# Unread TensorE products ahead of some stages in the first five and last four tiles of an RWKV and FP4 kernel

## What is computed

```python
h = _layernorm(x) * (1 + ca) + sa
for i in range(2):                              # _forward, two layers
    h = h + _time_mix(_ln(h, ln1_w), p)         # five mixes, r k v w g, a scan over tokens (wkv), group norm, Wo
    h = h + _channel_mix(_ln(h, ln2_w), p)      # relu(k @ cWk)^2 @ cWv, gated by sigmoid(r @ cWr)
x = x + ga * _ln(h, ln_out_w)
h = _layernorm(x) * (1 + cb) + sb
gate, y = fp4_linear(h, w_gate), fp4_linear(h, w_up)
x = x + gb * fp4_linear(silu(gate) * y, w_down) # operands quantized in blocks of 16
```

## Time and profile before

| | us |
|---|---|
| median of three runs | 3195.91 |
| lowest and highest | 3187.82, 3196.2 |
| the profiled execution, its own time | 3192.44 |
| its span, first to last instruction | 3190.7 |
| mean granted TensorE clock | 0.969 of full speed |

### The profile page before, as it was taken

The page is one execution under the profiler, slowest core; times in us unless marked ns, Lnnn a source line. Parts: engine busy times, 40 slices in busy tenths (PEclk is TensorE's granted clock), DMA queues, the critical chain, the costliest instruction groups (busy, mean ns, idle before and its releaser), DMA issues.

```text
span 3190.7 us, 79561 instructions
## 1 busy us (share of the span) xinstructions
PE 2926.2 (92%) x33341; PEld 2317.9 (73%) x33341; DVE 2383.7 (75%) x5345; ACT 1252.3 (39%) x2451; POOL 1270.3 (40%) x1456
## 2 busy tenths in 40 slices
PE   5589999999999999999999999999999999999875
PEld 3467777777777777777777777777777777777653
DVE  4646777887777788777778787777878777787654
ACT  1233444444344434434443444444443444344321
POOL 3234344444344444433444443344444434444320
PEclk7689999999999999999999999999999999999987
DMA  4000000000000000000000000000000000000000
GB/s 140 13 5 8 8 8 12 9 11 12 12 8 8 12 8 12 12 12 11 6 11 8 12 12 12 12 5 12 8 12 12 11 12 8 8 8 12 8 8 7
DMA packets 36313, 41.56 MB, mean 13 GB/s; under 512 B 2748, under 2 KB 34680, under 8 KB 35960
## 3 DMA queue, kind: packets, MB, share of 16 engines
q1 hardware_dynamic: 35696, 36.32, 3.6%
q10 hardware_dynamic: 264, 0.16, 0.0%
HBM read 28.08 MB, written 8.39 MB: 11 GB/s over the span
## 4 chain that ended last, share of the span: by engine, by line
PE 67%; DVE 13%; issue 11%; POOL 7%; ACT 2%; DMA 0%; DVEq 0%; ACTq 0%; POOLq 0%
PE ps_all L1087 11%; PE ps_all L1309 10%; PE ps_all L1095 7%; PE ps_all L1276 6%; PE ps_all L1290 6%; PE ps_all L1199 6%; PE ps_all L1328 5%; PE ps_all L1079 3%; PE ps_all L1126 2%; DVE sxrk L954 2%; POOL grstd L605 2%; DVE att L961 2%; PE ps_all L1320 2%; PE ps_all L1173 1%; POOL sxrk L568 1%
## 5 line engine op out<-in xcount | busy, mean ns | idle before, releaser
L581 POOL TENSOR_TENSOR mixin<-mixin,hT_tm 128x512 f32<-128x512 f32 x320 | 375.6, 1179 | 912.4 <-DVE mixin L920 910.3
L954 DVE TENSOR_TENSOR sxrk<-sxrk,dec 128x512 f32<-128x512 f32 x384 | 301.7, 786 | 217.0 <-PE ps_all L1199 214.4
L1276 PE MATMUL ps_all<-chan,cwk 128*128 128x256 f32 x1536 | 362.7, 386 | 3.0 <-DVE ffn_work L1015 3.0
L1290 PE MATMUL ps_all<-cwv,chan 128*128 128x256 f32 x1536 | 348.6, 383 | 0.0
L1199 PEld LDWEIGHTS ps_all<-sxrk 64*64 64x64 f32 x12288 | 223.0, 137 | 158.6 <-issue 158.4
L1199 PE MATMUL ps_all<-sxrk 64*64 64x32 f32 x12288 | 259.2, 223 | 72.0 <-DVE att L961 68.3
L1290 PEld LDWEIGHTS ps_all<-cwv,chan 128*128 128x128 f32 x1536 | 286.5, 190 | 41.7 <-DVE ffn_work L1015 1.0
L1276 PEld LDWEIGHTS ps_all<-chan,cwk 128*128 128x128 f32 x1536 | 284.7, 190 | 42.7 <-DVE ffn_work L1015 3.8
L920 DVE SCALAR_TENSOR_TENSOR mixin<-ps_all,vcol,sxrk 128x256 f32<-128x256 f32 x640 | 272.4, 476 | 25.6 <-PE ps_all L1130 14.6
L563 POOL TENSOR_TENSOR rstd<-var,powc 128x2 f32<-128x2 f32 x224 | 179.8, 803 | 201.5 <-DVE var L867 192.0
L961 DVE COPY_PREDICATED att<-masks,ps_all 128x256 f32<-128x256 uint8 x384 | 201.5, 525 | 9.3
(11 more groups left out here) (179 smaller groups left out, 6290.7 us busy)
## 6 DMA issues: line engine op xcount, KB each, us to landing
xin<-in_L_attn_x_dram SPq DMA_DIRECT2D x32, 256.0 KB, 2.7
tok<-in_L_attn_x_dram SPq DMA_DIRECT2D x32, 256.0 KB, 2.7
out_dram<-x SPq DMA_DIRECT2D x32, 256.0 KB, 2.1
cwk<-in_L_attn_cWk_dram SPq DMA_DIRECT2D x2, 768.0 KB, 7.9
cwv<-in_L_attn_cWv_dram SPq DMA_DIRECT2D x2, 768.0 KB, 10.0
ffn_work<-in_L_wmod_dram SPq DMA_DIRECT2D x2, 512.0 KB, 6.3
tok<-in_L_ffn_w_down_dram SPq DMA_DIRECT2D x1, 704.0 KB, 4.0
tok<-in_L_ffn_w_gate_dram SPq DMA_DIRECT2D x1, 640.0 KB, 7.6
```

The lines of the kernel that those rows point to most:

```text
L581: pool.tensor_tensor(m, m, hT["tm", l][:, :, :, 1:P + 1].rearrange("p k c t -> p (k c) t"), ALU.add).then_inc(ev["mixed"][b], 1)
L954: v.tensor_tensor(rko, rko, t, ALU.mult).then_inc(ev["rk_lev"][b], 1)
L1276: ins = pe.matmul(bank(b, "ck", lj, "k")[:, m * TT:(m + 1) * TT], cwk[:, l, k, n:n + P], k_in[:, k, :], start=(k == 0), stop=(k == KC - 1))
L1290: ins = pe.matmul(bank(b, "cv", l, "v")[:, c * D:(c + 1) * D], relu[t // 2][:, t % 2, c * P:(c + 1) * P], cwv[:, l, t, :], start=(t == 0), ...
```

## The change

`WAITING` names, for tiles 0 to 4 and for the last four, stages of PE and a number n for each. Before such a stage PE now waits for the bank as `fill` does and then issues n products of the 128 x 128 identity with itself into the first 128 columns of that bank. Nobody reads them: the stage that follows starts its own group in the same bank. For `lev.3`, `lev.5` and `lev.6` the bank is not the stage's own but that of `pg` or `kt`, the next stage that writes another bank. In all there are 659 such products: 144, 118, 67, 17 and 7 in tiles 0 to 4, and 4, 16, 93 and 193 in tiles 28 to 31. Nothing else is moved; the other engines' lists are the same.

```diff
+WAITING = {
+    0: """0 turn.tm 16; 0 mix 9; 0 mf.0 4; 0 pw1 7; 0 pk 2; ...
...
+    -1: """... 1 yt 12; 1 wo 8; ... 4 xt 61; 4 gu.0.0 3; 4 ht.0 23; 4 ht.1 23; 4 dn
...
-        def turns(eng, run, steps, meanwhile):
+        def turns(eng, run, steps, meanwhile, before=None):
             for i, b, kind, arg in run:
+                if before:
+                    before(i, b, kind, arg)
                 steps[kind](i, b, arg)
...
+            RESULT = {"lev.3": "pg", "lev.5": "kt", "lev.6": "kt"}
...
+            def unread(i, b, kind, arg):
+
+                name = stage_name(kind, arg)
+                n = count[i, b, name] if (i, b, name) in count else 0
+                if n:
+                    kind, arg, use = use_of[b, RESULT[name] if name in RESULT else name]
+                    fill(pe, i, b, kind, arg, use)
+                    for _ in range(n):
+                        pe.matmul(bank(b, kind, arg, use)[:, 0:P], ident[:, :], ident[:, :], start=True, stop=True)
...
-            turns(pe, RUN[PE], steps, meanwhile)
+            turns(pe, RUN[PE], steps, meanwhile, unread)
```

More of the change, by code:

```diff
@@ L45 @@
         4/4 dn; 0/0 mf.0; 4/3 lna.out; 1/2 st.0 st.1; 4/3 lna.ffn; 0/0 mf.1; 1/2 gnb; 0/0 mf.3""",
+}
+WAITING = {
+    0: """0 turn.tm 16; 0 mix 9; 0 mf.0 4; 0 pw1 7; 0 pk 2; 0 pr 3; 0 lev.3 4; 0 lev.5 5; 0 lev.6 3; 0 kt 2; 0 yt 11; 0 wo
+        7; 2 turn.cm 23; 2 ck.0 1; 1 pr 3; 1 lev.3 2; 1 lev.5 4; 1 lev.6 3; 1 kt 1; 1 yt 13; 1 wo 3; 3 turn.cm 8; 3 ck.0
+        3; 4 xt 3; 4 gu.0.0 1; 4 ht.0 2; 4 ht.1 1""",
+    1: """0 turn.tm 11; 0 mix 3; 0 mf.0 4; 0 pw1 4; 0 pk 13; 0 pr 3; 0 lev.3 3; 0 lev.5 5; 0 lev.6 3; 0 kt 2; 0 yt 11; 0
+        wo 3; 2 turn.cm 1; 1 pw1 13; 1 pr 3; 1 lev.3 2; 1 lev.5 4; 1 lev.6 3; 1 kt 1; 1 yt 13; 1 wo 3; 3 turn.cm 3; 3
+        ck.0 3; 4 xt 3; 4 gu.0.0 1""",
+    2: """0 turn.tm 1; 0 mix 3; 0 pw1 1; 0 pr 3; 0 lev.3 3; 0 lev.5 4; 0 lev.6 3; 0 kt 2; 0 wo 3; 1 turn.tm 2; 1 pw1 13; 1
+        pr 3; 1 lev.3 2; 1 lev.5 4; 1 lev.6 3; 1 kt 1; 1 yt 13; 1 wo 3""",
[4 rows of a table added]
+    -2: """1 turn.tm 2; 1 pw1 13; 1 pr 3; 1 lev.3 3; 1 lev.5 4; 1 lev.6 4; 1 kt 2; 1 yt 13; 1 wo 7; 3 turn.cm 5; 3 ck.0 4;
+        3 cv 2; 4 xt 4; 4 gu.0.0 2; 4 ht.0 4; 4 ht.1 19; 4 dn 2""",
+    -1: """0 lev.5 4; 0 kt 2; 0 wo 3; 2 ck.0 1; 1 turn.tm 2; 1 mix 3; 1 mf.0 2; 1 pw1 13; 1 pr 3; 1 lev.3 4; 1 lev.5 4; 1
+        lev.6 3; 1 kt 3; 1 yt 12; 1 wo 8; 3 turn.cm 3; 3 ck.0 8; 3 cv 2; 4 xt 61; 4 gu.0.0 3; 4 ht.0 23; 4 ht.1 23; 4 dn
+        3""",
 }
@@ L1073, in meanwhile @@
                     weights_turn(*TURNS_AT[at])
+            RESULT = {"lev.3": "pg", "lev.5": "kt", "lev.6": "kt"}
+            use_of = {}
+            for home in HOME:
+                use_of.setdefault((home[0], stage_name(home[1], home[2])), home[1:])
+            count = {}
+            for tile, text in WAITING.items():
+                for entry in text.split(";"):
+                    b, name, n = entry.split()
+                    count[tile % N, int(b), name] = int(n)
+            def unread(i, b, kind, arg):
[6 more added lines that the diff above has]
+                        pe.matmul(bank(b, kind, arg, use)[:, 0:P], ident[:, :], ident[:, :], start=True, stop=True)
             def turn_tiles(i, b, kind, arg, use, src):
```

## The result

| | before | after |
|---|---|---|
| median of four runs, us | 3195.14 | 3235.82 |
| lowest and highest, us | 3187.82, 3196.2 | 3234.4, 3239.41 |
| profiled execution: time, span, us | 3192.44, 3190.7 | 3239.41, 3237.7 |
| mean granted clock | 0.969 | 0.990 |

A forecast was written before the change was run, and what follows sets the result against it. The prediction took PE's work to bound the middle and a chain of waits between PE and the other engines the two ends. Profiled 3192.4 + 65 cost - 34 given back by the clock = 3223 us; range 3200 to 3250.

The forecast's parts named there:

- The bound: PE's work bounds the middle; at both ends a chain of PE and other engines waiting for each other does.
- The price: One unread product costs PE 0.22 us at full clock, 0.44 at the low clock; 659 products are 145.0 us.
- the rival with 0.38 by the weight load: Weight loads do not overlap, so each product costs 0.38 us: 3318 us in all; chance 0.05.
- The cost, 65 us: Of 145.0 us of products, 73.1 stand in no wait; less what is swallowed, 65 us reach the end.
- The further 5 us: Estimate of uncovered product time swallowed by later waits in the first two rounds and the drain, besides `pk` in tile 1.
- my table: Table by stretch of product time against PE's idle time: 71.9 us covered by waits, 73.1 not covered.
- The clock's gift, 34 us: Half-clock stretches turned full give back 34 of at most 60.7 us, mostly in the first 300 us and last stretch.
- The clock wins: All 19 half-clock stretches turn full, 60.7 us saved against 55 cost: 3187 us, or 3182; chance 0.10.
- The clock hardly moves: Most low stretches stay low, only the last tile gains, 10 us: 3247 us; chance 0.15.
- my mark of 0.985: Profile sign for the whole run: a mean granted clock of 0.985 would be half of the low time gone.
- The delays are swallowed: In the middle DVE works off its queue during products, so only 31 us are paid: 3189 us; chance 0.10.
- The Trainium skill's rule: Only long idle gaps lower the clock, so products in short waits save nothing: about 8 us less gift, 3231 us.

The follow-up runs named there:

- full_only: Only the change's 314 products between 190 and 3070 us, added to the kernel before: 3247.16 us, ratio 1.0162.
- middle13: None of the table's products; 13 products ahead of `pw1` of stream 1 in tiles 8 to 17, added to the kernel before: 3222.59 us, ratio 1.0091.
- start_only: Only the change's 165 products of the first two tiles, up to 190 us, added to the kernel before: 3182.32 us, ratio 0.9964.
- end_only: Only the change's 180 products after 3070 us, added to the kernel before: 3187.9 us, ratio 0.9982.
- clipped: The change's table with each number cut to what the old wait holds, 296 products instead of 659, against the kernel before: 3165.18 us, ratio 0.9915.
- end_long: Only 61, 23 and 23 products in the three long waits of the last tile, added to the kernel before: 3184.84 us, ratio 0.9971.

## Why the prediction was right

**The bound.** That PE's work bounds the middle and a chain the ends was right. full_only (+51.7 us) and middle13 (2.90 us a round for 13 products) show it.

**The price.** 0.22 us was right, 0.223 was measured; the rival with 0.38 by the weight load falls. What the term left out is that a product by itself costs 0.1 to 0.2 us more; the 17 such entries between 190 and 3070 us come to 2.8 us over their share.

**The cost, 65 us: too small.** Measured are 78.7 at the stages. Of those, the products ahead of `pk` and `pr` in tile 1 came back; elsewhere the stage starts show no more than 0.3 us at a time. PE in order of time there:

```profile
122.89 3.06 PE L1115 MATMUL ps_all<-ident 128*128 128x128 f32 x26
...
136.14 1.23 PE L1215 MATMUL ps_all<-decay_h,td_w 64*128 64x128 f32 x8 [4.25 <-DVE mixin L942]
```

The wait ahead of `pw2` is 4.25 us where it was 7.81: 3.56 us swallowed, as predicted for the 13 of `pk` (2.9). The further 5 us, my estimate for the rest, were not found. The term is thus 78.7 - 3.6 = 75, and was sized 10 us too small: about 5 from that estimate, the rest because less was covered than my table had. The largest part of that is in the full rounds: the 188 products between 190 and 440 us cost 42.6 us, 0.227 each, so that the 6.2 us (3.0 and 3.2) which my table has there as covered were not. I had counted many idle times of 0.1 to 0.2 us as cover, and no product fits into those. The end went the other way, +2.3 instead of 7.0. Products in half clock are dearer too. Tile 0 has some:

```profile
26.60 3.73 PE L1115 MATMUL ps_all<-ident 128*128 128x128 f32 x32
30.17 0.60 PE L1121 MATMUL ps_all<-ident,mixin 128*128 128x128 f32 x4
...
43.96 3.35 PE L1115 MATMUL ps_all<-ident 128*128 128x128 f32 x14 [6.05 <-DVE mixin L942]
47.24 1.12 PE L1181 MATMUL ps_all<-mixin,td_w 128*64 128x128 f32 x8
```

The 16 ahead of `turn.tm` delay the first transpose by 1.85 us (30.17 against 28.32 in the earlier trace rows). The 7 ahead of `pw1` wait 6.05 us for the bank and then run at half clock, 3.35 us, or 0.48 each: the wait that I had set them into had ended when the bank came free. That is 3.0 us at one entry. In tile 31, 8 products ahead of `ck.0` did the same, 3.60 us:

```profile
3147.52 3.60 PE L1115 MATMUL ps_all<-ident 128*128 128x128 f32 x16 [1.81 <-DVE ffn_work L1037]
```

**The clock's gift, 34 us: near in the sum, wrong in place.** The rest column has -31.8, of which 3.6 are the swallowed products, so the gift is about 28. I had given 9, 5, 4, 1 and 15; the column, with the 3.6 taken out of the second, has about 5, 7, 2, 7 (with 300 to 440 and from 2900 on) and 8. Cost and gift missed in the same direction, 10 and 6 us, and these make the 16 us between the forecast's +31 and the +46.9 of the profiled executions; what kept the measured time inside the range is its width. The largest miss of the whole ledger is the stretch from 190 to 300 us, +17.7 instead of +11.5. Of these 6.2 us, 3.9 are cost (19.4 instead of 15.5) and 2.2 the clock's gift (1.8 instead of 4). The latter shows at its head. Before and after, PE in order of time:

```profile
196.13 3.78 PE L1095 MATMUL ps_all<-wv,mixin 128*128 128x256 f32 x8
...
201.23 0.67 PE L1199 MATMUL ps_all<-sxrk 64*64 64x32 f32 x32 [1.31 <-DVE att L961]
```

```profile
191.47 1.99 PE L1137 MATMUL ps_all<-wv,mixin 128*128 128x256 f32 x8
...
197.36 0.67 PE L1241 MATMUL ps_all<-sxrk 64*64 64x32 f32 x32 [3.90 <-DVE att L983]
```

The clock is lifted as I had assumed, and Wv's products take 1.99 us instead of 3.78. But the wait for DVE ahead of `lev.2` grows from 1.31 to 3.90 us, so PE's lead shrinks from 4.66 us (196.13 - 191.47) to 3.87 (201.23 - 197.36) instead of growing by 1.8. In these microseconds DVE works through twelve groups of layer-norm instructions in a row, with no idle time shown between them, before it comes to the work for `lev.2` (L976, L978), and is the late one:

```profile
188.53 0.74 DVE L883 BATCH_NORM_STATS2 stats<-xres 128x6 f32<-128x256 f32 x2
...
194.93 0.17 DVE L889 TENSOR_SCALAR var<-mv 128x2 f32<-128x2 f32 x1
195.01 0.69 DVE L976 TENSOR_TENSOR sxrk<-sxrk,dec 128x512 f32<-128x512 f32 x1
195.62 0.72 DVE L978 COPY_PREDICATED att<-dmask,ps_all 128x512 f32<-128x512 uint8 x1
```

I had seen this for one place (32.8 to 41 us) and had not asked it of the others. Whether DVE's queue is what limits the gift everywhere in the first 300 us isn't shown; no run moved that queue.

**The end.** 3070 to the end is -5.9 where I had -8.0. That this is near is luck: the cost was a third of what I had (2.3, not 7.0) and the gift about half (8.2, not 15). PE in order of time in the last tile:

```profile
3170.98 4.40 PE L1115 MATMUL ps_all<-ident 128*128 128x128 f32 x38
...
3182.24 13.78 PE L1115 MATMUL ps_all<-ident 128*128 128x128 f32 x122
3196.20 0.63 PE L1121 MATMUL ps_all<-ident,ffn_work 128*128 128x128 f32 x4 [0.18 <-DVE ffn_work L439]
...
3197.61 1.42 PE L1351 MATMUL ps_all<-gateT,ffn_work 128*128 128x352 f32 x4
...
3203.39 5.40 PE L1115 MATMUL ps_all<-ident 128*128 128x128 f32 x46
...
3211.83 2.00 PE L1351 MATMUL ps_all<-gateT,ffn_work 128*128 128x352 f32 x4 [0.47 <-ACT ffn_work L770]
...
3227.67 5.35 PE L1370 MATMUL ps_all<-downT,ffn_work 128*128 128x256 f32 x24
```

The 61 products fill the wait of 13.78 us to within 0.18 us, the 19 (4.40 us) stand in one of 1.68 us, as predicted. The first `gu` runs at full clock, 1.42 us; a later one, at 3211.83, takes 2.00 again, since the clock fell once more at 3212.6 us. My mark "`gu` at 0.50 no more" was met in the first half only. `dn` runs in 5.35 us, where it took 7.95 before, by the same view of before:

```profile
3178.12 7.95 PE L1328 MATMUL ps_all<-downT,ffn_work 128*128 128x256 f32 x24 [0.67 <-ACT ffn_work L752]
```

**The rivals and marks.** The clock wins: refuted for this table by the middle's 52 us, though its mechanism holds at the ends (start_only, end_only) and in `clipped`. The clock hardly moves: refuted, two thirds of the low time are gone (200.6 to 64.7 us); the mean clock of 0.990 is above my mark of 0.985. So more clock was lifted than I thought, and less time came of it. The delays are swallowed: refuted by middle13. The round from `cv` to `cv` that began at 310.03 us takes 107.5 us instead of 92.7, the one from 402.71 takes 97.5, and behind the table's products the rounds are 92.7 again; my mark was some 10 us more. My mark for the busy time of the new line, near 145 us, reads 179.0 and says nothing against the price: it holds the tail of each of the 130 groups and the products in half clock. The lower end of the forecast's spread should have been 3202 (3192.4 + 60 - 50) and not 3205, which changes no chance. The Trainium skill's rule that long gaps are what matters, which I had weighed at 8 us, would have left a gift of 26 us; 28 were measured, nearer to it than to my 34. And end_long, with products in the long waits alone, did as well as end_only, so for the last tile the runs agree with it. Just ahead of it they don't. In before the clock falls at 3067.2 us, and no wait between 3030 us and there is longer than 1.84 us:

```profile
3059.91 0.74 PE L1199 MATMUL ps_all<-sxrk 64*64 64x32 f32 x32 [1.60 <-DVE att L961]
...
3066.58 0.67 PE L1199 MATMUL ps_all<-sxrk 64*64 64x32 f32 x32 [1.84 <-DVE att L961]
```

At the start short waits and long ones were filled together, and which of them lifted the clock was not taken apart; that stays open.

## What to carry to other kernels

Count every unread product against the wait behind a free bank, at its price (here 0.223 us), and put in no more than fits: in this kernel 296 such products won 0.85%, 659 lost 1.3%, at the same mean clock. Where TensorE bounded a stage, filler was paid in full and nothing later took it up; where DVE was late (at 190 us), the lifted clock turned into a longer wait. A mean granted clock alone therefore tells little of the time: look for the stretches at half clock in which TensorE itself is the late one.

## What the runs showed of the hardware beyond what was expected

Unread 32-bit transposes keep the granted clock up as products do (0.99 in the last 52 us, where it was 0.68 without them). Records of 128 moving columns start every 112 ns at full clock, weight load included; at half clock a product of two records took 0.45 us (3.60 for 8) to 0.48 (3.35 for 7). A product by itself costs 0.32 us or more and not 0.22. In before the clock fell at 3067.2 us, and PE had not been idle for more than 1.84 us at a time in the 37 us ahead of it. And single executions of before and middle13, whose first 440 us are the same program, were 5.3 us apart at 207 us, since their low stretches fell differently; a gain of that size can be read from medians of several runs only.
